# Second-layer attention of a two-layer block: one 32-row strip per head instead of a shared 96-row block

## The chip, the cores and the metric

The kernel runs on one core of a Trainium2 chip. The metric is the time on the device, in microseconds (us), of one execution. Before the change three timed runs gave 1500.37, 1506.84 and 1507.55 us, median 1506.84.

## The reference

The input x has 2048 rows of 128. Four stages follow each other, each added to its input and normalised over the last axis (a layer norm without parameters):

```python
x = LN(x + attn0(x))   # 8 query heads, 2 key groups, causal, latent size 32 per group
x = LN(x + ffn0(x))    # gated FFN, 352 wide, FP4 quantise-dequantise in blocks of 16
x = LN(x + attn1(x))   # below
x = LN(x + ffn1(x))    # 8 experts, weighted by a thresholded softmax
# attn1: H, G, HD = 16, 4, 8
q = (x @ Wq.T + bq).reshape(b, n, G, 4, HD)
k = (x @ Wk.T + bk).reshape(b, n, G, HD)
v = (x @ Wv.T + bv).reshape(b, n, G, HD)
attn = softmax(einsum('bqghd,bkgd->bghqk', q, k) / sqrt(HD))   # not causal
y = einsum('bghqk,bkgd->bqghd', attn, v).reshape(b, n, d) @ Wo.T + bo
```

attn1 has 16 heads of 8 numbers; four heads share the keys of one group. All 2048 queries see all 2048 keys.

## The kernel before

Work goes by chunks of 512 queries (QC) and by key group: a first-layer iteration is (chunk, one of 2 groups), a second-layer iteration (chunk, one of 4 groups), each with four heads. Within an iteration the keys go by tiles of 128. For each tile and head there is a unit: a score matmul (L710) makes scores transposed, 128 keys by 512 queries, in one of three PSUM banks; ScalarE takes the exponential to PR (L903); a product matmul (L728) multiplies by the values, in which a column of ones sums the weights. In the second layer four heads write their products to four strips of 32 rows of one bank, so products come in fours; the trace shows each float32 product as two records. Four units of one key tile with their products are one repeating piece, 16 of them an iteration.

The exponential needs the row maximum. It is found beforehand: for each head, query tile and chunk of keys a matmul (L637, 128 queries by 512 keys) fills one of four side banks, and VectorE reduces it to one column of MP (L1134): 64 such maxima for a second-layer iteration. row_max reduces them further (L1212), a transpose (L642) and a copy bring them to MR, and a DMA (L552) writes them into the last row of the query operand, against which the keys have a row of ones. So the score matmul subtracts the maximum by itself.

For accuracy keys and queries are in two parts, high (rounded to f32r, one pass through TensorE) and low (what is left). The contraction is over high x high, low x high and high x low parts, 3 x 32 rows. In the second layer a group's four heads share the 32 key rows: KO1 holds the 8 key numbers repeated for the four heads, in three parts, 96 rows and the row of ones. A head's own queries are QO rows of its 8 numbers in each part, with the other heads' rows made zero by a mask: q_all (L632) makes all queries of a chunk, ScalarE and VectorE split them to QH and QL (L821, L1123), VectorE copies the group's rows to QB (L1220), and GpSimd multiplies by the head's mask into the query buffer (L968, L971). Queries have four buffers; the fourth lies in KO0, which the second layer no longer needs.

The order of work is written out once as a list of steps (`steps0`, `steps1`, `iteration`, `stream`), and each engine walks the same list in order, with semaphores between them. In an iteration's list each score is followed by the next items beside it: maxima of the coming iteration (it begins a quarter of an iteration after the present one's start and goes on so ahead of its use), and the steps of the FFN or the experts of an earlier chunk. The part list is walked for layer 0, for second-layer chunk 0, in a hardware loop for chunks 1 and 2 (L509), and for chunk 3. The last first-layer iteration and the stretch after it, in which the last chunk's FFN runs, carry the maxima of the first second-layer iterations.

At the start GpSimd fills buffers with constants, among them the rows of ones of KO0 and KO1 (L956, L958), while SyncE issues the loads one by one.

Of the kernel before, what the change touches and what calls it, by code (L numbers as in the profile page):

```python
# [18 lines left out]
P = 128  # L19
T = 2048  # L20
D = 128
NT = T // P
QC = 512
NC = T // QC
QT = QC // P
# [23 lines left out]
CONST_W = 4 * P + 12  # L49


def constants():

    c = np.zeros((P, CONST_W), np.float32)
    i = np.arange(P)
    c[:, 0:P] = np.eye(P)
    c[:, P:2 * P] = np.where(i[:, None] > i[None, :], NEG, 0.0)
    c[:, 2 * P:3 * P] = np.where(i[None, :] > i[:, None], NEG, 0.0)
    for h in range(HG):
        c[:, 3 * P + h] = (i < SHIFT) & ((i % LAT) // HD1 == h)  # L60
    c[:, 3 * P + 4:3 * P + 8] = -0.5
    return c


def build(nc, A):
# [3 lines left out]
    with ctx:  # L69
# [11 lines left out]
        ident, head_mask, minus_half = const[:, 0:P], const[:, 3 * P:3 * P + 4], const[:, 3 * P + 4:3 * P + 8]  # L81
# [6 lines left out]
        KO1 = sb("KO1", [KR, G1, T], f32r)  # L88
        QO = sb("QO", [KR, 3, HG, QC], f32r)

        QBUF = [QO[:, b, :, :] for b in range(3)] + [KO0[:, 0, :].rearrange("p (h q) -> p h q", h=HG)]
        QB = sb("QB", [SHIFT, QC], f32r)
# [46 lines left out]
        WQ1T, WO1T = sb("WQ1T", [P, D]), sb("WO1T", [P, D])  # L139
        QH = sb("QH", [P, QC], f32r)  # L140
        QL = sb("QL", [P, QC], f32r)
        WKV1T = sb("WKV1T", [P, 2 * LAT])
        WK13 = sb("WK13", [P, G1, SHIFT])
        bq = sb("bq", [P, 1])
        bk3 = sb("bk3", [SHIFT, G1])
# [39 lines left out]
        q_base = sem("q_base")  # L185
# [78 lines left out]
        KO = (KO0, KO1)  # L264
# [3 lines left out]
        IN_PARTS = ("q0", "k0", "k1", "q_all")  # L268
        QUANTS = ("quant_x", "quant_h", "quant_w")
        BY_VECTOR = ("norm0", "quant_w", "stats", "final", "q1") + MADE  # L270
# [52 lines left out]
        def stream(part, with_queries=True):  # L323
# [4 lines left out]
            for entry in part:  # L328
# [4 lines left out]
                if with_queries:  # L333
                    asked = (([("q_all", c)] if layer else keys0(c)) if g == 0 else []) + queries(layer, c, g, it)
# [13 lines left out]
        def steps0():  # L348
# [10 lines left out]
            for i, (_, c, g, it) in enumerate(part):  # L359
                beside = between(work, cuts[i], cuts[i + 1]) if i < len(part) - 1 else []  # L360
                if i == len(part) - 1:

                    begun = [step for _, step in behind[1:QUANT_STAGES]]
                    beside = [("q_all", 0)] + begun[:2] + maxima(1, 0, 0, 0, range(NC - 2))
                    begun, behind = begun[2:4] + queries(1, 0, 0, 0) + begun[4:], behind[:1] + behind[QUANT_STAGES:]
# [53 lines left out]
        def name_of(item):  # L419
# [4 lines left out]
            return (kind, item[3]) if kind == "q0" else (kind,)  # L424

        def needs(step):

            kind = step[0]
            if kind == "max":
                _, layer, h, q, kc, c, g, b = step  # L430
                return [("q0", b), ("k0", g)] if layer == 0 else [("k1", g)]
# [5 lines left out]
                    "k1": [("x2T",), ("w1T",)], "v1": [("x2T",)], "q_all": [("x2T",), ("w1T",)],  # L437
# [18 lines left out]
        class Count:  # L456


            def __init__(self, steps):
# [9 lines left out]
                self.groups = kinds.count("q0") + kinds.count("q1")  # L469
                self.bases = kinds.count("q1")  # L470
# [5 lines left out]
            def plus(self, other, times=1):  # L476
# [10 lines left out]
                new.bases = self.bases + other.bases * times  # L487
# [16 lines left out]
        def parts(engine, walk):  # L504
# [4 lines left out]
            with engine.Fori(1, NC - 1) as c:  # L509
# [5 lines left out]
        def _(sp):  # L515
# [15 lines left out]
            sp.dma_start(bq[:, :], A["L1_attn_bq"].rearrange("(r o) -> r o", o=1)).then_inc(ld["attn1"], 16)  # L531
            for r in range(3):
                for j in range(HG):
                    sp.dma_start(bk3[r * LAT + j * HD1:r * LAT + (j + 1) * HD1, :],
                                 A["L1_attn_bk"].rearrange("(g r) -> r g", g=G1), allow_slow_non_contiguous=True).then_inc(ld["attn1"], 16)
# [29 lines left out]
        N_ATTN1 = 16 * (4 + 1 + 3 * HG + 2)  # L565
# [3 lines left out]
        def _(pe):  # L569
            def side_item(item, n, k):  # L570
# [26 lines left out]
                elif kind in ("k0", "k1"):  # L597
                    g, c = item[1:]
                    w = WK3 if kind == "k0" else WK13
                    last = nc.tensor.matmul(bank[0:SHIFT, :], w[:, g, :], XT[:, c * QC:(c + 1) * QC],  # L600
                                            start=True, stop=True)
# [5 lines left out]
                elif kind == "v1":  # L607
                    for j in range(QT):
                        t = item[1] * QT + j
                        last = nc.tensor.matmul(bank[:, j * LAT:(j + 1) * LAT], XT[:, t * P:(t + 1) * P],  # L610
                                                WKV1T[:, LAT:2 * LAT], start=True, stop=True)
# [17 lines left out]
                elif kind == "q_all":  # L629
                    c = item[1]  # L630
                    src = XT[:, c * QC:(c + 1) * QC] if isinstance(c, int) else XT[:, bass.ds(c * QC, QC)]
                    last = nc.tensor.matmul(bank[:, :], WQ1T[:, :], src, start=True, stop=True)  # L632
                elif kind == "max":
                    layer, h, q, kc, c, g, buf = item[1:]
                    n = (q + 1) * P if layer == 0 and kc == c else QC
                    causal = layer == 0 and kc == c
                    last = nc.tensor.matmul(bank[:, 0:n], QBUF[buf][0:SHIFT, h, q * P:(q + 1) * P],  # L637
                                            KO[layer][0:SHIFT, g, kc * QC:kc * QC + n], start=True, stop=not causal)
# [63 lines left out]
            def scores(step, n, u):  # L702
# [7 lines left out]
                m = nc.tensor.matmul(dst[:, q0:QC], KO[layer][:, g, kt * P:(kt + 1) * P], QBUF[buffer_of(layer, it)][:, h, q0:QC],  # L710
# [618 lines left out]
```

## Time and profile before

| | |
|---|---|
| Timed runs | 1500.37, 1506.84, 1507.55 us |
| Span of the profiled execution (no time around it is given) | 1503.6 us |
| Mean granted TensorE clock | 0.937 |
| PE busy (matmul) | 1367.3 us, 91% |
| DVE (VectorE) busy | 1098.1 us, 73% |
| ACT (ScalarE) busy | 827.1 us, 55% |
| POOL (GpSimd) busy | 126.5 us, 8% |

The second layer's attention begins at 634 us of the span and ends at 1463 us; 1415 to 1463 us is its last iteration, where no maxima are left to find. A line of the profile such as L710 is a line of the kernel. PE is the matmul side of TensorE and PEld its weight loads, which overlap. Matmuls are pipelined, so a matmul's duration is longer than the time until the next can begin: the distance between starts tells what one costs. "Idle" before an instruction is the time its engine stood still, and the name behind the arrow is what ended it.

### The profile page before, as it was taken

What the parts mean: (1) busy time and instruction counts of PE and PEld (TensorE: products, weight loads), DVE (VectorE), ACT (ScalarE), POOL (GpSimd) and SP (SyncE); (2) the same over time, 40 slices, a digit from 0 to 9 for tenths busy, and PEclk for the clock granted to TensorE, in tenths of its full rate; (3) what the DMA queues carried; (4) which work ended last, traced back from release to release, by engine and by line L of the source; (5) the groups of instructions that cost most, each with busy time, mean ns of one, the idle gap of its engine ahead of it and who ended that gap; (6) DMA issues with size and microseconds to landing.
All of it is one profiled execution on the core that took longest, in us unless ns stands there. A gap on an engine that the chain in (4) does not pass through costs nothing.

```text
span 1503.6 us, 20967 instructions
## 1 busy us (share of the span) xinstructions
PE 1367.3 (91%) x6537; PEld 697.0 (46%) x6537; DVE 1098.1 (73%) x2178; ACT 827.1 (55%) x1589; POOL 126.5 (8%) x159
## 2 busy tenths in 40 slices
PE   4788899989998965799999999999999999999994
PEld 2444445344433433445555554554554555554432
DVE  4667687678745678778788888887889887887424
ACT  2435534564456511266676666666666666667760
POOL 3000000000000010000000112000121000000033
PEclk9769899899999975799999999999999999999996
DMA  3000000000000000000000000000000000000000
GB/s 101 1 1 1 1 1 2 1 1 1 1 0 1 0 1 0 1 1 1 2 1 1 1 1 9 1 2 3 1 2 8 1 2 2 1 1 1 1 1 14
DMA packets 8785, 6.43 MB, mean 4 GB/s; under 512 B 2072, under 2 KB 7904, under 8 KB 8672
## 3 DMA queue, kind: packets, MB, share of 16 engines
q1 hardware_dynamic: 8672, 5.04, 1.2%
q8 instruction: 57, 0.93, 0.3%
q14 instruction: 56, 0.46, 0.1%
HBM read 3.79 MB, written 1.05 MB: 3 GB/s over the span
## 4 chain that ended last, share of the span: by engine, by line
PE 79%; DVE 13%; ACT 3%; issue 3%; POOL 1%; DMA 0%; DVEq 0%; POOLq 0%; ACTq 0%
PE ps L728 24%; PE ps L710 24%; PE ps L637 19%; DVE MP L1134 6%; PE ps L696 2%; PE ps L600 2%; ACT QO L804 1%; PE ps L663 1%; PE ps L645 1%; PE ps L674 1%; ACT PR L903 1%; PE ps L627 1%; PE ps L648 1%; PE ps L652 1%; PE ps L713 1%
## 5 line engine op out<-in xcount | busy, mean ns | idle before, releaser
L1134 DVE TENSOR_REDUCE MP<-ps 128x1 f32<-128x512 f32 (+2 forms) x1344 | 827.8, 665 | 218.8 <-PE ps L637 185.8
L903 ACT ACTIVATE PR<-ps 128x512 f32<-128x512 f32 (+2 forms) x1344 | 702.0, 584 | 469.8 <-PE ps L710 366.8
L710 PE MATMUL ps<-QO,KO 97*128 97x512 f32 (+3 forms) x1088 | 473.6, 445 | 26.2 <-ACT PR L903 18.3
L637 PE MATMUL ps<-KO,QO 96*128 96x512 f32 (+2 forms) x1088 | 450.1, 437 | 30.8 <-DVE MP L1134 13.1
L728 PE MATMUL ps<-PR,V 128*32 128x512 f32 (+2 forms) x2688 | 432.2, 600 | 0.6 <-ACT OS L804 0.5
L710 PEld LDWEIGHTS ps<-QO,KO 97*128 97x128 f32 x1088 | 208.4, 194 | 339.8 <-ACT PR L903 235.6
L637 PEld LDWEIGHTS ps<-KO,QO 96*128 96x128 f32 x1088 | 219.6, 204 | 91.3 <-DVE MP L1134 39.1
L728 PEld LDWEIGHTS ps<-PR,V 128*32 128x32 f32 (+1 forms) x2688 | 73.7, 115 | 137.5 <-issue 72.0
L710 PE MATMUL ps<-KO 97*128 97x512 f32 x256 | 105.4, 434 | 2.7 <-ACT PR L903 1.5
L637 PE MATMUL ps<-KO 96*128 96x512 f32 x256 | 99.1, 396 | 0.0
L710 PEld LDWEIGHTS ps<-KO 97*128 97x128 f32 x256 | 46.9, 189 | 68.6 <-ACT PR L903 58.1
L963 POOL TENSOR_TENSOR RS<-VE,const 128x4 f32<-128x4 f32 x16 | 16.2, 1013 | 523.1 <-DVE VE L1067 523.1
L968 POOL TENSOR_TENSOR QO<-QB,const 96x512 fp32r<-96x512 f32 x12 | 12.8, 1067 | 530.9 <-DVEq L1223 530.9
L637 PEld LDWEIGHTS ps<-KO 96*128 96x128 f32 x256 | 48.6, 190 | 9.1 <-DVE MP L1134 1.2
L1117 DVE TENSOR_TENSOR QO<-ps,QO 32x512 fp32r<-32x512 f32 x32 | 22.0, 688 | 27.1 <-ACT QO L804 22.8
L980 POOL TENSOR_TENSOR qa<-qa 128x512 f32<-128x512 f32 (+2 forms) x24 | 19.7, 821 | 170.7 <-DVE XQ L1179 166.1
L696 PE MATMUL ps<-ew,XQT 128*128 128x512 f32 x64 | 33.4, 620 | 0.0
L640 PE MATMUL ps<-mask_qk,ident_b 128*128 128x128 bf16 x128 | 33.4, 261 | 0.0
L713 PE MATMUL ps<-mask_kq,ident_b 128*128 128x128 bf16 x128 | 31.8, 248 | 0.0
L804 ACT ACTIVATE HQT<-ps 128x256 f32<-128x256 f32 (+2 forms) x36 | 11.0, 355 | 34.2 <-PE ps L669 31.3
L600 PE MATMUL ps<-XT,WK 128*96 128x512 f32 x48 | 28.7, 700 | 0.0
L669 PE MATMUL ps<-const,H 128*128 128x128 f32 (+1 forms) x48 | 9.8, 319 | 16.2 <-DVEq L1057 15.5
(177 smaller groups left out, 792.0 us busy)
## 6 DMA issues: line engine op xcount, KB each, us to landing
result<-OUT SPq DMA_DIRECT2D x4, 256.0 KB, 2.3
H<-in_L_attn_wq SPq DMA_DIRECT2D x1, 512.0 KB, 6.9
HQT<-in_L_attn_wo SPq DMA_DIRECT2D x1, 512.0 KB, 5.1
ew<-in_L_ffn_expert_w SPq DMA_DIRECT2D x1, 512.0 KB
QO<-MR SPq DMA_DIRECT2D x20, 8.0 KB, 1.8
const<-in_consts SPq DMA_DIRECT2D x1, 262.0 KB, 2.8
bk<-in_L_attn_bk SPq DMA_DIRECT2D x12, 0.1 KB
wd<-in_L_ffn_w_down SPq DMA_DIRECT2D x1, 176.0 KB, 3.6
```

Source lines behind the costliest of these rows:

```text
L600: last = nc.tensor.matmul(bank[0:SHIFT, :], w[:, g, :], XT[:, c * QC:(c + 1) * QC], start=True, stop=True)
L637: last = nc.tensor.matmul(bank[:, 0:n], QBUF[buf][0:SHIFT, h, q * P:(q + 1) * P], KO[layer][0:SHIFT, g, kc * QC:kc * QC + n], start=True, ...
L640: last = nc.tensor.matmul(bank[:, n - P:n], ident_b[:, :], mask_qk[:, :], start=False, stop=True)
L696: last = nc.tensor.matmul(bank[:, :], X2T[:, q * P:(q + 1) * P], ew[:, 4 * e:4 * e + 4, :], start=True, stop=True)
L710: m = nc.tensor.matmul(dst[:, q0:QC], KO[layer][:, g, kt * P:(kt + 1) * P], QBUF[buffer_of(layer, it)][:, h, q0:QC], start=True, stop=not ...
L713: m = nc.tensor.matmul(dst[:, q0:q0 + P], ident_b[:, :], mask_kq[:, :], start=False, stop=True)
L728: nc.tensor.matmul(dst, VO[layer][:, kt, g, :], PR[:, u % NP_RING, q0:QC], start=kt == 0, stop=kt == key_tiles(layer, c) - 1).then_inc(pv_ ...
L804: return nc.scalar.activation(out, in_, ACT.Copy)
L903: nc.scalar.activation(PR[:, u % NP_RING, q0:QC], ps[:, 8 - nb + u % nb, q0:QC], ACT.Exp, scale=SCALE[layer]).then_inc(exp_done, 1)
L980: nc.gpsimd.tensor_tensor(t[:, 0:w, :], t[:, 0:w, :], t[:, w:2 * w, :], ALU.add).then_inc(pool_chain, 1)
L1117: i = v.tensor_tensor(q[2 * LAT:SHIFT, :], bank[h * LAT:(h + 1) * LAT, :], q[0:LAT, :].bitcast(f32), ALU.subtract)
L1134: v.tensor_reduce(MP[:, buf, h, q, kc:kc + 1], bank[:, 0:w], AX, ALU.max).then_inc(free, 1)
```

## The change

Each second-layer head gets a strip of 32 partitions of its own, in keys (KO1, now 128 rows) and in queries (Q1, 128 rows by 4 groups): 8 numbers in three parts, 24 rows, and a 25th row for the ones (keys) and the shift (queries). The weights WK13 and WQ13 are laid out so that one matmul per group makes all four strips; ScalarE writes the high parts and zeros (a per-partition scale of 0 or 1), VectorE the tails. A maximum contracts 24 rows of its strip, a score 25. The maxima of the second layer are emitted with the head innermost. The masked queries, QB, QH, QL and q_all go; q1 becomes a step of its own per group, with a bank. The shift goes by four DMAs, one a strip. The bias comes by 24 small DMAs. The hardware loop over chunks 1 and 2 is written out.

```diff
-CONST_W = 4 * P + 12
+PARTS1 = 3 * HD1
+ROWS1 = PARTS1 + 1
+CONST_W = 3 * P + 10
...
+    c[:, 3 * P + 4] = (i % LAT) // HD1 == 1
+    c[:, 3 * P + 5] = (i % LAT) // HD1 == 2
+    c[:, 3 * P + 6:3 * P + 10] = (i % LAT == PARTS1)[:, None]
...
-        KO1 = sb("KO1", [KR, G1, T], f32r)
+        KO1 = sb("KO1", [P, G1, T], f32r)
+        Q1 = sb("Q1", [P, G1, QC], f32r)
...
-            return [("max", layer, h, q, kc, c, g, buffer_of(layer, it)) for h in range(HG) for q in range(QT)
-                    for kc in chunks or range(top)]
+            if layer == 1:
+                return [("max", 1, h, q, kc, c, g, it) for q in range(QT) for kc in chunks or range(NC) for h in range(HG)]
...
-            with engine.Fori(1, NC - 1) as c:
+            for c in range(1, NC - 1):
...
-                        dst = QBUF[step[3]][SHIFT:KR, :, :].rearrange("o h (q p) -> o (h q) p", p=P)
-                        sp.dma_start(dst.bitcast(f32), MR[:, :].bitcast(f32)).then_inc(shifted, 16)
+                            for h in range(HG):
+                                row = h * LAT + PARTS1
+                                dst = Q1[row:row + 1, step[3], :].rearrange("o (q p) -> o q p", p=P)
+                                sp.dma_start(dst.bitcast(f32), MR[h * QT:(h + 1) * QT, :].bitcast(f32)).then_inc(shifted, 16)
...
+                elif kind == "q1":
+                    g, c, _ = item[1:]
+                    last = nc.tensor.matmul(bank[:, :], WQ13[:, g, :, :], XT[:, c * QC:(c + 1) * QC], start=True, stop=True)
+                elif kind == "max" and item[1] == 1:
+                    _, h, q, kc, c, g, buf = item[1:]
+                    rows = slice(h * LAT, h * LAT + PARTS1)
+                    last = nc.tensor.matmul(bank[:, :], Q1[rows, buf, q * P:(q + 1) * P], KO1[rows, g, kc * QC:(kc + 1) * QC],
+                                            start=True, stop=True)
...
-                m = nc.tensor.matmul(dst[:, q0:QC], KO[layer][:, g, kt * P:(kt + 1) * P], QBUF[buffer_of(layer, it)][:, h, q0:QC],
-                                     start=True, stop=not causal)
+                    rows = slice(h * LAT, h * LAT + ROWS1)
+                    m = nc.tensor.matmul(dst[:, :], KO1[rows, g, kt * P:(kt + 1) * P], Q1[rows, it, :], start=True, stop=True)
...
+                        i = nc.scalar.activation(Q1[:, item[3], :], bank, ACT.Identity, bias=bq_low[:, g:g + 1], scale=low_q)
...
+                        i = nc.scalar.activation(KO1[:, item[1], item[2] * QC:(item[2] + 1) * QC], bank, ACT.Identity,
+                                                 bias=bk_low[:, item[1]:item[1] + 1], scale=low_k)
...
+            nc.gpsimd.memset(WQ13[:, :, :, :], 0.0)
+            nc.gpsimd.memset(WK13[:, :, :, :], 0.0)
...
-            nc.gpsimd.memset(KO1[SHIFT:KR, :, :].bitcast(f32), 1.0).then_inc(ones_set, 1)
+            nc.gpsimd.memset(UNUSED[:, :], 0.0).then_inc(ones_set, 1)
...
-            def masked(n, buf):
-
-                pool.wait_ge(q_base, n)
-                nc.gpsimd.tensor_tensor(QBUF[buf][0:SHIFT, 0, :], QB[:, :].bitcast(f32),
-                                        head_mask[0:SHIFT, 0:1].broadcast_to([SHIFT, QC]), ALU.mult)
...
+                    tails(KO1[:, item[1], item[2] * QC:(item[2] + 1) * QC], bank, bk13[:, item[1]:item[1] + 1]).then_inc(free, 1)
+                elif kind == "q1":
+                    tails(Q1[:, item[3], :], bank, bq13[:, item[1]:item[1] + 1]).then_inc(free, 1)
...
-                    for part, src in enumerate((QH, QH, QL)):
-                        i = v.tensor_scalar(QB[part * LAT:(part + 1) * LAT, :], src[g * LAT:(g + 1) * LAT, :].bitcast(f32),
-                                            1.0, None, ALU.mult)
```

## Rows read from the trace of the kernel before

**Rows 1.** The page, busy us (share of the span) and count by engine.
```profile
PE 1367.3 (91%) x6537; PEld 697.0 (46%) x6537; DVE 1098.1 (73%) x2178; ACT 827.1 (55%) x1589; POOL 126.5 (8%) x159
```
**Rows 2.** Stretches: length, busy PE, PEld, DVE, ACT, POOL, clock, DMA share, GB/s.
```profile
650.00:1415.00 765.00, 753.84 (x3930) 388.57 (x3925) 628.32 (x1107) 508.05 (x982) 68.04 (x89) 1.00 0.01 2
...
534.00:640.00 106.00, 68.44 (x203) 40.09 (x202) 81.92 (x188) 17.82 (x32) 5.07 (x6) 0.67 0.00 0
```
**Rows 3.** The chain of waits, 650 to 1463 us, shares by line.
```profile
by line: PE ps L710 32.9%; PE ps L728 29.2%; PE ps L637 24.8%; DVE MP L1134 3.1%; PE ps L696 2.5%; issue 1.8%; PE ps L645 0.7%; ACT PR L903 0.5%; DVE QB L1220 0.5%; PE ps L692 0.4%; PE ps L656 0.3%; DVE ST L1062 0.3%; PE ps L632 0.3%; PE ps
```
**Rows 4.** By shape, 650 to 1415 us: count | busy us, mean ns | idle.
```profile
L1134 DVE TENSOR_REDUCE MP<-ps 128x1 f32<-128x512 f32 x909 | 566.6, 684 | 112.0 <-PE ps L637 108.2
L903 ACT ACTIVATE PR<-ps 128x512 f32<-128x512 f32 x941 | 494.9, 600 | 247.5 <-PE ps L710 243.9
```
**Rows 5.** Timeline (start us, length us) of a piece with four maxima.
```profile
1244.15 1.06 PE L728 MATMUL ps<-PR,V 128*32 128x512 f32 x8
...
1245.15 0.50 PE L710 MATMUL ps<-KO 97*128 97x512 f32 x1
...
1245.49 0.40 PE L637 MATMUL ps<-KO,QO 96*128 96x512 f32 x1
...
1245.92 1.89 DVE L1134 TENSOR_REDUCE MP<-ps 128x1 f32<-128x512 f32 x3 [0.21 <-PE ps L637]
...
1246.89 0.39 PE L637 MATMUL ps<-KO,QO 96*128 96x512 f32 x1
...
1247.21 0.64 PE L728 MATMUL ps<-PR,V 128*32 128x512 f32 x4
```
**Rows 6.** Timeline of a piece without maxima.
```profile
1459.78 1.07 PE L728 MATMUL ps<-PR,V 128*32 128x512 f32 x8
...
1460.78 0.98 PE L710 MATMUL ps<-KO 97*128 97x512 f32 x3
...
1461.97 0.50 PE L710 MATMUL ps<-KO 97*128 97x512 f32 x1 [0.21 <-ACT PR L903]
...
1462.40 1.06 PE L728 MATMUL ps<-PR,V 128*32 128x512 f32 x8
```
**Rows 7.** DVE, 650 to 1463 us: stretch of L1220 alone, then L1123.
```profile
650.00:1463.00 813.00, 16.31 (x39) 1.00 0.01 2
...
L1123 DVE SCALAR_TENSOR_TENSOR QL<-ps,bq,QH 128x512 fp32r<-128x512 f32 x3 | 2.3, 751 | 3.0 <-ACT QH L821 3.0
```
**Rows 8.** By shape, whole span; then L632's matmuls, min/median/max ns.
```profile
L1081 DVE SCALAR_TENSOR_TENSOR KO<-ps,bk,KO 32x512 fp32r<-32x512 f32 x16 | 11.9, 743 | 10.8 <-ACT KO L828 9.2 <-PE ps L600 1.2
...
L632 PE MATMUL ps<-XT,WQ1T x6: 590/592/595, 730.4 to 1168.5; 128*128 x4, 128*128 128x512 f32 x2
```
**Rows 9.** What DVE waited for, 650 to 1415 us: total, times, longest.
```profile
DVE MP L1134 <- PE ps L637: 108.2, 187, 3.2
```
**Rows 10.** Timeline of the start.
```profile
8.52 6.96 POOL L958 MEMSET KO<- 1x8192 f32 x1
...
11.70 4.96 DVE L1305 COPY WK<-wkd 128x32 f32<-128x32 f32 x6
...
16.98 1.94 PE L584 MATMUL ps<-const,H 128*128 128x128 f32 x8 [7.60 <-DVEq L1306]
```
**Rows 11.** Timeline at the loop's edge and at the last shift.
```profile
1048.83 0.49 PE L710 MATMUL ps<-QO,KO 97*128 97x512 f32 x1 [2.68 <-issue]
...
1413.49 0.50 SPq L552 DMA_DIRECT2D KO<-MR  x1
1415.30 0.53 PEld L710 LDWEIGHTS ps<-KO 97*128 97x128 f32 x3 [2.05 <-DMA KO<-MR]
```
**Rows 12.** Timeline of PE from 634 us.
```profile
634.28 0.76 PE L710 MATMUL ps<-QO,KO 97*128 97x512 f32 x1 [1.37 <-DVE UNUSED L1142]
634.85 0.63 PE L637 MATMUL ps<-KO,QO 96*128 96x512 f32 x1
635.27 0.63 PE L710 MATMUL ps<-QO,KO 97*128 97x512 f32 x1
```

More of the change, by code:

```diff
@@ L333, in stream @@
                 if with_queries:
-                    asked = (([("q_all", c)] if layer else keys0(c)) if g == 0 else []) + queries(layer, c, g, it)
+                    asked = (keys0(c) if layer == 0 and g == 0 else []) + queries(layer, c, g, it)
                 lead = before * QUERY_LEAD
@@ L363, in steps0 @@
                     begun = [step for _, step in behind[1:QUANT_STAGES]]
-                    beside = [("q_all", 0)] + begun[:2] + maxima(1, 0, 0, 0, range(NC - 2))
-                    begun, behind = begun[2:4] + queries(1, 0, 0, 0) + begun[4:], behind[:1] + behind[QUANT_STAGES:]
+                    beside = queries(1, 0, 0, 0) + begun[:2] + maxima(1, 0, 0, 0, range(NC - 2))
+                    begun, behind = begun[2:], behind[:1] + behind[QUANT_STAGES:]
                 yield from iteration(0, c, g, beside, behind, outs, carry, it, begun)
@@ L430, in needs @@
                 _, layer, h, q, kc, c, g, b = step
[L431 removed]
+                return [("q0", b), ("k0", g)] if layer == 0 else [("q1", b), ("k1", g)]
             return {"fold_q": [("wqT", 0), ("wqT", 1), ("wupT",)], "fold_o": [("wupT",)],
@@ L468, in __init__ @@
                 self.outs = kinds.count("out_copy")
-                self.groups = kinds.count("q0") + kinds.count("q1")
-                self.bases = kinds.count("q1")
+                self.groups = kinds.count("q0")
                 self.shifts = kinds.count("shift")
@@ L530, in _ @@
             sp.dma_start(Wkv1[LAT:2 * LAT, :], A["L1_attn_Wv"]).then_inc(ld["attn1"], 16)
[L531 to L535, printed above, removed]
+            sp.wait_ge(consts_set, 1)
+            for h in range(HG):
+                for r in range(3):
+                    rows = slice(h * LAT + r * HD1, h * LAT + (r + 1) * HD1)
+                    sp.dma_start(bq13[rows, :], A["L1_attn_bq"].rearrange("(g h d) -> h d g", g=G1, h=HG)[h],
+                                 allow_slow_non_contiguous=True).then_inc(ld["attn1"], 16)
+                    sp.dma_start(bk13[rows, :], A["L1_attn_bk"].rearrange("(g d) -> d g", g=G1),
+                                 allow_slow_non_contiguous=True).then_inc(ld["attn1"], 16)
             for dst, name, n in ((bv_b, "L1_attn_bv", LAT), (bo_b, "L1_attn_bo", D)):
@@ L628, in side_item @@
                                             start=True, stop=True)
[L629 to L632, printed above, removed]
+                elif kind == "q1":
[5 more added lines that the diff above has]
+                    last = nc.tensor.matmul(bank[:, :], Q1[rows, buf, q * P:(q + 1) * P], KO1[rows, g, kc * QC:(kc + 1) * QC],
+                                            start=True, stop=True)
                 elif kind == "max":
                     layer, h, q, kc, c, g, buf = item[1:]
[L635 to L638, printed above, removed]
+                    n = (q + 1) * P if kc == c else QC
+                    causal = kc == c
+                    last = nc.tensor.matmul(bank[:, 0:n], QO[0:SHIFT, buf, h, q * P:(q + 1) * P],
+                                            KO0[0:SHIFT, g, kc * QC:kc * QC + n], start=True, stop=not causal)
                     if causal:
@@ L709, in scores @@
                 dst = ps[:, 8 - nb + u % nb, :]
-                m = nc.tensor.matmul(dst[:, q0:QC], KO[layer][:, g, kt * P:(kt + 1) * P], QBUF[buffer_of(layer, it)][:, h, q0:QC],
-                                     start=True, stop=not causal)
+                if layer == 0:
+                    m = nc.tensor.matmul(dst[:, q0:QC], KO0[:, g, kt * P:(kt + 1) * P], QO[:, buffer_of(0, it), h, q0:QC],
+                                         start=True, stop=not causal)
+                else:
+                    rows = slice(h * LAT, h * LAT + ROWS1)
+                    m = nc.tensor.matmul(dst[:, :], KO1[rows, g, kt * P:(kt + 1) * P], Q1[rows, it, :], start=True, stop=True)
                 if causal:
@@ L768, in walk @@
                             its += 1
-                            pe.wait_ge(shifted, 16 * (n.iterations + its + 1))
+                            pe.wait_ge(shifted, 64 * (n.iterations + its + 1))
                         scores(step, n, u)
@@ L777, in walk @@
                         pe.wait_ge(out_free, n.outs + outs)
-                    if kind == "max" and step[7] in q_at:
+                    if kind == "max" and step[1] == 0 and step[7] in q_at:
                         pe.wait_ge(q_ready, q_at.pop(step[7]))
@@ L991, in walk @@
                         rstd(n.rstd + rs)
-                    if kind == "q1":
-                        bases += 1
-                        masked(n.bases + bases, step[3])
                     if kind in ("expert", "ebias"):
@@ L1074, in normalise, with tails @@
                 return i
-            def tails(dst, tail, bank, bias=None):
-                lo = slice(tail * LAT, (tail + 1) * LAT)
-                if bias is None:
-                    return v.tensor_tensor(dst[lo, :], bank[lo, :], dst[lo, :].bitcast(f32), ALU.subtract)
-                return v.scalar_tensor_tensor(dst[lo, :], bank[lo, :], bias[lo, :], dst[lo, :].bitcast(f32), ALU.add,
-                                              ALU.subtract)
+            def tails(dst, bank, bias):
+                return v.scalar_tensor_tensor(dst, bank, bias, dst.bitcast(f32), ALU.add, ALU.subtract)
             def chunk_of(c):
```

119 lines of the change are left out of this document (54 added, 65 removed).

## Prediction

> **What bounds the kernel now.** I read the page first, then the second layer alone, then one repeating piece of it instruction by instruction. The page has TensorE (PE) at 91% and VectorE (DVE) at 73% [rows 1]. The change touches the second-layer attention, so the stretches come next [rows 2]: from 650 to 1415 us, where the maxima of coming queries run beside the scores, PE is busy 753.8 of 765 us at full clock, DVE 628.3, ScalarE (ACT) 508.1. The chain of waits over 650 to 1463 us is PE almost alone: scores (L710) 32.9%, products (L728) 29.2%, maxima (L637) 24.8%; the DVE reduction has 3.1% [rows 3]. So PE bounds this layer, and DVE is next, 137 us behind.
>
> The stretch has 941 exponentials, one per score unit, hence 235 pieces of four units ("quads": four scores, some maxima, four products), 765/235 = 3.26 us each; its 909 reductions make 3.9 a quad [rows 4]. One quad with four maxima [rows 5]: products start at 1244.15, the first score at 1245.15 (1.00 us later), its neighbour 0.34 later, then a score or maximum each 0.233 us (1245.49 to 1246.89 are six such steps), and products again at 1247.21, 0.32 after the last maximum: 3.06 us, and nothing in it waits. The reader is to see that eight score and maximum matmuls cost PE about 1.9 us, although each contracts 96 or 97 rows of which a head's own are 24.
>
> **The change, part by part.**
>
> *Strips.* After it, a score or maximum uses the 32 rows of its head's strip, and the emission order of the maxima puts the four heads next to each other. Does PE run strips side by side? The trace has no matmul that contracts a strip. It has the other direction: products write 32 output rows each, and four records take 0.64 us, eight 1.06 [rows 5], so four run together. Bounds for one S or M matmul in a strip: 0.233 us as now (no overlap; gain nothing), down to a quarter of it, 0.06. Scores walk heads 0 to 3, maxima too but at a shifted phase, so in the worst case a maximum sits behind a score of its own strip and pairs with the next score: five steps of 0.233 for eight matmuls, 1.17 us. I take overlap, anywhere from pairs to fours; PE then needs at most 1.00 + 0.34 + 3 x 0.233 + 0.32 = 2.4 us a quad, and it stops being the bound.
> The Trainium skill (TensorE: Matmul & The Clock Gate, Part 3: Packing small matmuls) says that matmuls in different 32-row strips run concurrently, four of them 3.07 times as fast; by it the eight would cost 8 x 0.233/3.07 = 0.6 us, an estimate from that page. No row here shows it; it speaks against the second rival below.
>
> *What is late next.* Two things. First the loop between PE and ACT: a score needs one of three banks. The quad without maxima shows it bare [rows 6]: products at 1459.78, three scores from 1460.78, the fourth at 1461.97 after 0.21 us of idle on the first exponential, products at 1462.40: 2.62 us. Row strips don't shorten this, so 2.62 is the floor of every quad. Second DVE: three reductions in 1.89 us with 0.68 for the last, so one each 0.60 us [rows 5]; four are 2.4 us, five 3.0.
> DVE's own work changes too. The three copies per group to QB (L1220: 16.3 us in this layer) and the QL tails (3 x 0.75 = 2.3) go [rows 7]; one tail per group comes, 13 x 0.74 at the price of the key tail L1081 [rows 8] = 9.7. So 628.3 - 16.3 - 2.3 + 9.7 = 619.4 us, 2.64 a quad: the two limits are equal on average, and the time lies above both because maxima come unevenly. DVE idles 137 us now, 108.2 of it waiting for a maximum [rows 9]. The other 28.5 (side chains through PE, ACT, GpSimd) stay. The uneven part I estimate: at 3.9 on average with threes, fours and fives, about a quarter of the quads (60) carry three maxima or fewer; DVE then idles 2.62 - 3 x 0.60 - 0.2 (side work) = 0.6 us, 60 x 0.6 = 36, and 4 us for quads whose other side matmuls hold PE. Sum 619.4 + 28.5 + 40 = 688, against 765: **-77 us**. Ends: 0 (no overlap), and -146 (DVE never idle).
>
> *1415 to 1463 us*, no maxima, 16 quads at 3.0 us: they are at the floor or hold expert matmuls with all 128 rows. -2 (0 to -6).
>
> *Query production.* GpSimd's four masking operations per group go; GpSimd is busy 68 of 765 us [rows 2], so that is worth nothing. The masked queries' wait goes; what is next is the DVE tail, a quad early at least. PE does 16 query matmuls instead of 4, each two records of 0.59 us [rows 8], begun 0.43 apart as such two-pass records are (the products' second four end 0.42 after the first) [rows 5]: +12 x 0.86 = 10 us of PE; ACT +12 at the length of an exponential, 0.60 [rows 4], is 7. Both now have slack under DVE; each can hold up a quad a little. +2 (0 to +10).
>
> *Switching between array shapes.* Layer 1's maxima are also issued in the last first-layer iteration and from 534 to 640 us, between matmuls that use 128 rows. The one shape change that the trace shows costs 0.32 - 0.233 = 0.09 us on entry to the products [rows 5]. Some 110 maxima, two changes each, 20 us of PE at most; from 534 to 640 PE is busy 68 of 106 us and DVE 82 [rows 2], which hides nearly all. +2 (0 to +20).
> The Trainium skill (TensorEngine Tiling (Array Packing), Key Properties) has the rule against this change: changing the tiling mode drains TensorE. The trace agrees as far as the 0.09 us goes. The products already differ in shape from the scores, so inside the layer the number of changes a quad stays two; by the rule the extra ones are those just priced.
>
> *Start.* The memset of 8192 ones on GpSimd (6.96 us) goes, two of 512 columns come, by the same price 6.96/16 = 0.44 each, and two tiny ones, 1 us. While it runs, six small copies of DVE take 4.96 us; PE waits 7.60 us for the last of them [rows 10]. The copies begin at 11.70; without the memset beside them I take 0.2 us each, an estimate, so they end near 13 instead of 16.7: -4 (0 to -5). The additional bias DMAs (24 for 13) are waited for only after this.
>
> *Loop unrolled.* At 1048.83 PE had stood 2.68 us with nothing to wait for [rows 11], once; -2 (0 to -3).
>
> *Four shift DMAs for one.* SyncE issues each in 0.50 us; exposed only where the last group's shift is late (issued 1413.49, score 1415.30) [rows 11]: 3 x 0.5 = +1.5. Elsewhere a shift has a quarter of an iteration ahead of its use.
>
> Sum: -77 - 2 + 2 + 2 - 4 - 2 + 1.5 = -79.5, on a span of 1503.6 us: 1424. The page gives no time around the span; the median of the timed runs, 1506.84, is 3.2 above it. Predicted 1427 us.
>
> **The rivals.**
> 1. *DVE becomes the bound, as above*: 1427, own range 1385 to 1465. For it: DVE is the only engine close behind. Chance 72%.
> 2. *The change doesn't do what it says*: strips are computed one after another. Then every S and M still costs 0.233, PE stays the bound, only the start, loop, added query matmuls and switches count: -4 - 2 + 10 + 2 + 1.5 = +7, with DVE's relief worth nothing: 1514, or 1504 if the added matmuls hide. For it: no row shows strips overlapping. Against: products overlap by columns. 10%.
> 3. *Partial gain through one queue*: PE issues in order, so a maximum waiting for DVE holds the next score back, and that score's exponential comes late. Both loops then add up in part, and a quad costs some 3.1 us instead of 2.93: 235 x 0.15 = 35 gained, 1469 with the small terms, up to 1490. For it: score and maximum alternate in the queue. Against: four side banks cover 4 x 0.60 = 2.4 us, more than the 1.3 us of products. 9%.
> 4. *Slower: the clock falls.* Throughout 650 to 1463 us PE is busy and the granted clock is 1.00 (2.4 GHz); from 534 to 640, where PE idles a third of the time, it is 0.67 on average [rows 2]. After the change PE would work perhaps 1.9 of 2.9 us. At 1.2 GHz a step is 0.42 us (634.85 to 635.27) and the first after a pause 0.57 (634.28 to 634.85) [rows 12]; the products' 1.00 would be 1.9, twice its 0.85 of streaming, and the 0.32 after the last maximum 0.5, both estimates. A quad in pairs: 1.9 + 0.57 + 3 x 0.42 + 0.5 = 4.2 us, against 2.93. It decides from (3.26 - 2.93)/(4.2 - 2.93) = a quarter of the quads on; at half of them, 235 x (0.5 x 1.27 - 0.33) = +72, some 1576 with the small terms. Against: a slow PE is a fully busy one, and from 650 us on the clock is full though the stretch ahead was not [rows 2]. 9%.
>
> **How the numbers follow.** Faster by over 0.5% (about what a measurement of this kernel can tell from no change): case 1, case 3 and a third of case 2, 84%. Within 0.5%: most of the rest of case 2, 6%. Slower: case 4 and a little of case 2, 10%. The range for 8 in 10 runs from 1385 (more than half of the way to DVE never idle) to 1490, which takes in case 3.
>
> **What would show it.** Maxima and scores starting a few ns apart in groups, at durations near 0.4 us; DVE near 90% busy where it was 82%, its waits for maxima from 108 to some 40 us; L637 and L710 gone from the head of the chain in favour of the reduction; quads without maxima still at 2.62 us; PE clock 1.00; PE's start on the weights near 13 us. The forecast is wrong if scores and maxima keep a pitch of 0.23 us, if the clock line shows halves after 650 us, or if DVE still waits over 80 us for maxima with PE idle.

## The result: 15.8% slower, at a lower TensorE clock

The changed kernel takes 1759.84 us (median of four runs: 1742.04, 1744.34, 1775.35, 1780.00) where the one before has 1505.49 (four runs). The ratio is 1.158, 95% interval 1.154 to 1.161; ratios here leave out runs well above the fastest of the same kernel, which are the two longer ones here (granted clock 0.68 where the others have 0.71), 1525.95 and 1530.01 us in e7 below, and 3654.64 us in e8. The forecast was 1427 us. What happened is rival 4, the falling clock, to which I gave 9%.

The page of the changed kernel, busy times by engine, its slices (tenths, 40 of them over the span) and the chain by line:

```profile
PE 1549.5 (89%) x6565; PEld 578.7 (33%) x6565; DVE 1081.3 (62%) x2149; ACT 840.0 (48%) x1602; POOL 71.6 (4%) x99
...
PE   4889899999997679999889999999999999998895
...
PEclk8688898999998566555775655655565565578586
...
PE ps L747 30%; PE ps L730 19%; ACT PR L921 7%; PE ps L726 5%; DVE MP L1138 4%; PE ps L652 4%; PE ps L646 3%; PE ps L711 3%; PE ps L642 2%; PE ps L660 1%; ACT QO L823 1%; PE ps L678 1%; PE ps L611 1%; PE ps L689 1%; POOL qc L990 1%
```

Against [rows 1], PE is busy 182 us longer with the same number of matmuls, give or take 28. Read alone, that says that PE is slower. The PEclk line says where. A slice is 43.5 us. In the first 13 slices, up to 566 us, it is 8 or 9 but for one 6; from there on it is 5 to 7 but for two slices of 8 near the end. The second layer begins at some 640 us; the stretch just ahead of it is at a low clock in both kernels (0.67 before, 0.65 after). (Products are now L747, scores of the second layer L730, its maxima L646, the reduction L1138.)

The stretches answer to [rows 2]: length, busy PE, PEld, DVE, ACT, POOL, granted clock, DMA share, GB/s.

```profile
650.00:1415.00 765.00, 717.29 (x3052) 214.96 (x3050) 482.92 (x845) 398.27 (x763) 27.43 (x36) 0.60 0.01 2
...
534.00:640.00 106.00, 69.89 (x208) 36.36 (x206) 80.61 (x183) 17.15 (x31) 2.01 (x2) 0.65 0.00 1
...
855.00:880.00 25.00, 20.79 (x153) 6.22 (x149) 22.71 (x38) 19.49 (x39) 0.00 (x0) 1.00 0.01 1
680.00:850.00 170.00, 161.74 (x642) 44.55 (x640) 94.33 (x156) 85.90 (x166) 0.00 (x0) 0.52 0.00 1
...
1541.00:1599.00 58.00, 49.52 (x346) 16.60 (x346) 50.96 (x86) 44.95 (x88) 0.00 (x0) 1.00 0.01 1
```

The same 765 us hold 763 ScalarE instructions where they held 982 [rows 2]. The clock is 0.60 where it was 1.00. The last three rows are the key: in the 25 us from 855, at full clock, DVE is busy 91%, as forecast (near 90%); in the 170 us from 680, at 0.52, it is 55%. The longest stretch at full clock, 58 us from 1541, has DVE at 88%; PE is busy only 85% of it, and the clock stays full.

A quad at full clock and one at half, from the timeline (start us, length us). First full:

```profile
1588.79 1.06 PE L747 MATMUL ps<-PR,V 128*32 128x512 f32 x8
1589.79 0.49 PE L730 MATMUL ps<-Q,KO 25*128 25x512 f32 x1
1589.79 0.50 PE L646 MATMUL ps<-KO,Q 24*128 24x512 f32 x1
1589.79 0.53 PE L730 MATMUL ps<-Q,KO 25*128 25x512 f32 x2
1590.12 0.40 PE L646 MATMUL ps<-KO,Q 24*128 24x512 f32 x2
1590.97 0.49 PE L730 MATMUL ps<-Q,KO 25*128 25x512 f32 x1 [0.44 <-ACT PR L921]
1591.38 1.07 PE L747 MATMUL ps<-PR,V 128*32 128x512 f32 x8
```

Then half:

```profile
1103.03 1.94 PE L747 MATMUL ps<-PR,V 128*32 128x512 f32 x8
1104.90 0.80 PE L730 MATMUL ps<-Q,KO 25*128 25x512 f32 x3
1105.49 0.64 PE L646 MATMUL ps<-KO,Q 24*128 24x512 f32 x3
1106.38 0.79 PE L730 MATMUL ps<-Q,KO 25*128 25x512 f32 x1 [0.25 <-ACT PR L921]
1107.10 1.08 PE L747 MATMUL ps<-PR,V 128*32 128x512 f32 x4
```

In the first, three scores and a maximum begin in one moment (1589.79) and last 0.5 us: strips do run side by side. The quad, with three maxima, is 2.59 us long, and PE stands still 0.44 us on ACT. In the second, three scores last 0.80 us together and three maxima 0.64, PE stands still 0.25 us on ACT, and products begin at 1103.03 and again at 1107.10, 4.07 us apart. Counted on the timeline over the whole second layer, from one set of products to the next: 67 quads at full clock with a mean of 2.87 us, 160 at half with 4.69, 27 with a change inside. Counted in the same way, the kernel before has 253 of 254 at full clock, with a mean of 3.24 us.

### The profile page after: what moved, and what is told of

It reads as the page before. It is cut to its first block, busy times and chain, and to the rows that moved or that the text cites. A ratio compares the mean times of both kernels' runs of the same rounds, so it can differ in the third digit from the quotient of the medians.

```text
span 1740.3 us, 19160 instructions
## 1 busy us (share of the span) xinstructions
PE 1549.5 (89%) x6565; PEld 578.7 (33%) x6565; DVE 1081.3 (62%) x2149; ACT 840.0 (48%) x1602; POOL 71.6 (4%) x99
## 4 chain that ended last, share of the span: by engine, by line
PE 76%; DVE 10%; ACT 9%; issue 3%; POOL 1%; DMA 1%; SPq 1%; DVEq 0%; POOLq 0%; ACTq 0%
PE ps L747 30%; PE ps L730 19%; ACT PR L921 7%; PE ps L726 5%; DVE MP L1138 4%; PE ps L652 4%; PE ps L646 3%; PE ps L711 3%; PE ps L642 2%; PE ps L660 1%; ACT QO L823 1%; PE ps L678 1%; PE ps L611 1%; PE ps L689 1%; POOL qc L990 1%
## 5 line engine op out<-in xcount | busy, mean ns | idle before, releaser
L1138 DVE TENSOR_REDUCE MP<-ps 128x1 f32<-128x512 f32 (+2 forms) x1344 | 827.6, 664 | 389.7 <-PE ps L646 306.8
L747 PE MATMUL ps<-PR,V 128*32 128x512 f32 (+2 forms) x2688 | 585.4, 839 | 0.6 <-ACT OS L823 0.6
L730 PE MATMUL ps<-Q,KO 25*128 25x512 f32 x1024 | 412.6, 668 | 68.6 <-ACT PR L921 60.8
L646 PE MATMUL ps<-KO,Q 24*128 24x512 f32 x1024 | 411.8, 635 | 16.6 <-DVE MP L1138 12.7
L730 PEld LDWEIGHTS ps<-Q,KO 25*128 25x128 f32 x1024 | 157.9, 253 | 578.6 <-issue 297.6
L646 PEld LDWEIGHTS ps<-KO,Q 24*128 24x128 f32 x1024 | 170.9, 262 | 55.2 <-DVE MP L1138 36.6
L726 PE MATMUL ps<-QO,KO 97*128 97x512 f32 (+3 forms) x320 | 148.8, 475 | 20.5 <-ACT PR L921 18.4
L652 PE MATMUL ps<-KO,QO 96*128 96x512 f32 (+2 forms) x320 | 137.1, 465 | 16.4 <-DVE QO L1120 13.0
L747 PEld LDWEIGHTS ps<-PR,V 128*32 128x32 f32 (+1 forms) x2688 | 81.5, 133 | 161.8 <-ACT PR L921 104.9
L726 PEld LDWEIGHTS ps<-QO,KO 97*128 97x128 f32 x320 | 63.9, 203 | 148.7 <-ACT PR L921 91.2
L652 PEld LDWEIGHTS ps<-KO,QO 96*128 96x128 f32 x320 | 69.0, 221 | 29.7 <-DVE QO L1120 14.1
L642 PE MATMUL ps<-XT,WQ 128*128 128x512 f32 x32 | 30.6, 1056 | 0.0
```

The lines of the kernel that those rows point to most:

```text
L642: last = nc.tensor.matmul(bank[:, :], WQ13[:, g, :, :], XT[:, c * QC:(c + 1) * QC], start=True, stop=True)
L646: last = nc.tensor.matmul(bank[:, :], Q1[rows, buf, q * P:(q + 1) * P], KO1[rows, g, kc * QC:(kc + 1) * QC], start=True, stop=True)
L652: last = nc.tensor.matmul(bank[:, 0:n], QO[0:SHIFT, buf, h, q * P:(q + 1) * P], KO0[0:SHIFT, g, kc * QC:kc * QC + n], start=True, stop=not ...
L726: m = nc.tensor.matmul(dst[:, q0:QC], KO0[:, g, kt * P:(kt + 1) * P], QO[:, buffer_of(0, it), h, q0:QC], start=True, stop=not causal)
L730: m = nc.tensor.matmul(dst[:, :], KO1[rows, g, kt * P:(kt + 1) * P], Q1[rows, it, :], start=True, stop=True)
L747: nc.tensor.matmul(dst, VO[layer][:, kt, g, :], PR[:, u % NP_RING, q0:QC], start=kt == 0, stop=kt == key_tiles(layer, c) - 1).then_inc(pv_ ...
```

## The experiments

Each is the changed kernel with one edit unless it says otherwise. The table gathers what they say of the clock. "Stretch" is 650 to 1415 us; "PE busy" is out of its 765 us.

| run | second-layer matmuls | span us | PE busy | clock in the stretch |
|---|---|---|---|---|
| before | 96 and 97 rows, one after another | 1503.6 | 753.8 | 1.00 |
| e5 | before, 64 rows | 1828.3 | 760.1 | 0.62 |
| e3 | before, 32 rows | 2006.5 | 761.7 | 0.57 |
| after | strips of 24 and 25 rows | 1740.3 | 717.3 | 0.60 |
| e4 | strips, maxima in the old order | 1839.8 | 755.8 | 0.56 |
| e9 | strips, 2 zero matmuls of 32 rows a quad | 1545.1 | 741.7 | 0.82 |
| e11 | same, 128 rows, 32 output rows | 1514.0 | 745.5 | 0.95 |
| e6 | same, 1 over the whole array | 1566.5 | 715.8 | 0.85 |
| e1 | same, 2 over the whole array | 1502.5 | 733.6 | 0.98 |
| e2 | same, 4 over the whole array | 1582.1 | 741.5 | 1.00 |

**e1_fill2, e2_fill4, e6_fill1: work for the whole array.**

```diff
+        FILL = sb("FILL", [P, P + QC], bf16)          # weights 0.0, moving data 1.0
...
+                if layer == 1 and h == 3 and kt != 1 and (c, g, kt) != (0, 0, 0):
+                    for _ in range(2):                # e6: 1, e2: 4
+                        nc.tensor.matmul(ps[:, OUT_BANKS[0], :], FILL[:, 0:P], FILL[:, P:P + QC], start=False, stop=False)
```

> The changed kernel with two matmuls of zero weights over all 128 rows (128x128 by 128x512, bfloat16) added before every fourth score of the second layer; they add zero to the output bank. Theory A (the second layer is slow because TensorE is granted 1.2 GHz while its matmuls use one strip each, and for nothing else): the clock returns to near 1.00 from 650 us on, a quad takes 2.8 to 3.0 us, span 1430 to 1490 us. Theory B (the clock falls because TensorE stands still between its matmuls, waiting for ScalarE and VectorE, whatever rows it uses): the same, since the idle time is filled; told from A by the rows run below. Theory C (strips and changes of array shape cost time by themselves, the clock is a side effect): 240 x 2 x 0.43 us more than the changed kernel, about 1900 us.

> As before, with four such matmuls before every fourth score. Theories A and B: clock 1.00, but four cost 0.9 us where some 0.45 us of slack stands before the fourth score, so a quad is about 3.2 us and the span 1500 to 1540 us, slower than with two if two suffice. Theory C: above 2000 us.

> The changed kernel with one zero matmul over all rows before every fourth score instead of two. If the work of the rows sets the grant, one is between none (0.57) and two (0.98): clock 0.75 to 0.95 in 650 to 1415 us, span 1520 to 1620 us. If one is enough, a quad is as long as with two or 0.1 us shorter, span 1480 us.

Measured, one run each: 1504.3, 1583.9 and 1568.3 us, beside 1508.4 us (one run, for the first two) and 1507.0 us (median of 15, for the third) for the kernel before. Adding about 480 matmuls that compute nothing takes 238 us off the span. This is the experiment that settles what slowed the change: the clock goes from 0.60 to 0.98 and the time with it. The stretch in e1:

```profile
650.00:1415.00 765.00, 733.63 (x4436) 239.74 (x4509) 626.39 (x1100) 533.06 (x1023) 28.48 (x37) 0.98 0.01 2
```

A quad with two of them, at full clock:

```profile
1227.20 1.06 PE L751 MATMUL ps<-PR,V 128*32 128x512 f32 x8
1228.20 0.49 PE L734 MATMUL ps<-Q,KO 25*128 25x512 f32 x1
...
1228.87 0.61 PE L725 MATMUL ps<-FILL 128*128 128x512 bf16 x2
1229.40 0.49 PE L734 MATMUL ps<-Q,KO 25*128 25x512 f32 x1
...
1230.07 1.06 PE L751 MATMUL ps<-PR,V 128*32 128x512 f32 x8
```

They stand where PE waited for ACT: the fourth score begins 1.20 us after the first, and did so after 1.18 in the full-clock quad without them. This quad, with two of its five maxima beside the fourth score, is 2.87 us. With four the clock is full, but its 247 full-clock quads have a mean of 3.45 us against the 3.24 of the kernel before, so e2 is 75 us slower than that one, and my 1500 to 1540 us was missed. With one, the clock is 0.85, within the 0.75 to 0.95 expected: full-clock quads have a mean of 2.95 us (193 of 254), and 45 at half clock with 5.15 lose it. Theory C, that shapes or strips are slow by themselves, falls. My figure for e1, 1430 to 1490, was missed: quads that carry experts, transposes or a query projection already fill PE, and there the zero matmuls only add. Counted on e1's timeline, its 242 full-clock quads have a mean of 3.08 us, where the kernel before has 3.24; of the other 12, six at half clock have a mean of 6.3 us and six with a change inside 5.0.

**e3_rows32 and e5_rows64: the old kernel with fewer rows.**

```diff
-                    last = nc.tensor.matmul(bank[:, 0:n], QBUF[buf][0:SHIFT, h, q * P:(q + 1) * P],
-                                            KO[layer][0:SHIFT, g, kc * QC:kc * QC + n], start=True, stop=not causal)
+                    kr = 32 if layer == 1 else SHIFT      # e5: 64; scores alike
+                    last = nc.tensor.matmul(bank[:, 0:n], QBUF[buf][0:kr, h, q * P:(q + 1) * P],
+                                            KO[layer][0:kr, g, kc * QC:kc * QC + n], start=True, stop=not causal)
```

> The kernel before, with the second layer's maxima and scores contracting only rows 0 to 31 (the low parts and the shift are left out). All lie in the same strip, so nothing overlaps and TensorE is as busy in time as before, 0.233 us a matmul. Theory A (the grant goes by how many rows of the array work): the clock falls from 1.00 to about 0.5 to 0.7 after 650 us, span 1700 us or more, even above the changed kernel, since nothing overlaps: 8 x 0.43 + 1.9 = 5.3 us a quad if always at 1.2 GHz. Theory B (it goes by the time in which TensorE stands still): TensorE never waits, the clock stays 1.00, span 1500 us.

> The kernel before, with the second layer's maxima and scores contracting rows 0 to 63 (the second low part and the shift are left out). Time per matmul is as before, 0.233 us at full clock, nothing overlaps. If the grant goes by how many rows of the array work, 64 lie between 96 (clock 1.00) and 32 (0.57 in 650 to 1415 us): I expect 0.8 to 1.0 there, span 1500 to 1700 us. If only matmuls confined to one 32-row strip count less, it is 1.00 and 1500 us.

Measured, one run each, 2008.3 and 1830.2 us, beside 1508.4 and 1507.0. The number, order and columns of the matmuls are those of the kernel before. What is contracted differs in content too: the low parts (in e5 one of them) and the row of the shift are left out. Zeros in the array don't lower the clock, as e1 with its zero weights shows, so I take the number of rows as the cause. Where the clock is full, a step costs what it did (e3, timeline):

```profile
1245.03 0.39 PE L638 MATMUL ps<-KO 32*128 32x512 f32 x1
1245.26 0.38 PE L712 MATMUL ps<-QO,KO 32*128 32x512 f32 x1
```

and yet over the stretch (e3):

```profile
650.00:1415.00 765.00, 761.73 (x2399) 357.92 (x2398) 409.64 (x685) 341.11 (x600) 44.83 (x59) 0.57 0.00 1
```

PE is busy 761.7 of 765 us, and is granted 1.2 GHz for most of it. So a fully occupied instruction stream doesn't hold the clock; how many rows its matmuls use counts. Weight loads don't explain it either: PEld is busy 357.9 us in e3, at a clock of 0.57, and 239.7 us in e1, at 0.98. The Trainium skill (TensorE: Matmul & The Clock Gate, section What's actually happening) says that the clock gate is set by how busy the PE has been; here the measurement decides that busy by the trace's rows is not the quantity. For e5 I had written 0.8 to 1.0 or, by the other reading, 1.00; both are missed, 64 rows gave 0.62, so it isn't proportional to rows.

**e9_fill2_strip and e11_fill2_cols: which part of the array.** The zero matmuls of e1 on FILL[0:LAT] only, and on all rows with 32 output rows (shortened).

```diff
-  nc.tensor.matmul(ps[:, OUT_BANKS[0], :], FILL[:, 0:P], FILL[:, P:P + QC], ...)
+  nc.tensor.matmul(ps[:, OUT_BANKS[0], :], FILL[0:LAT, 0:P], FILL[0:LAT, P:P + QC], ...)      # e9
+  nc.tensor.matmul(ps[0:LAT, OUT_BANKS[0], :], FILL[:, 0:LAT], FILL[:, P:P + QC], ...)        # e11
```

> The changed kernel with two zero matmuls before every fourth score as in the run with two over all rows, same columns and same place, but contracting only 32 rows (the first strip). They fill TensorE's time in the same way. If the grant goes by how many rows work, the clock stays where the changed kernel has it (0.5 to 0.65 in 650 to 1415 us) and the time is that of the changed kernel plus 240 x 2 x 0.3 to 0.43 us: 1850 to 1950 us. If it goes by TensorE's idle time, the clock comes back to near 1.00 as with all rows, 1500 us.

> The changed kernel with two zero matmuls before every fourth score that contract all 128 rows but make only 32 output rows (a quarter of the array's columns, as the products do). With all rows and columns two gave a clock of 0.98 in 650 to 1415 us, with 32 rows and all columns 0.82, with none 0.60. If a matmul counts by the part of the array it fills, rows times columns, this gives 0.82 as the 32-row ones do, span 1540 us. If only the rows count, 0.98 and 1500 us. If it is the time filled that counts, all three should have been alike, which they are not.

Measured, one run each, 1546.9 and 1515.8 us, beside 1508.4 and 1506.0. The stretch in e9:

```profile
650.00:1415.00 765.00, 741.68 (x4191) 243.92 (x4187) 595.37 (x1045) 488.39 (x943) 28.43 (x37) 0.82 0.01 2
```

and in e11:

```profile
650.00:1415.00 765.00, 745.50 (x4449) 235.46 (x4441) 622.25 (x1087) 524.71 (x1007) 28.47 (x37) 0.95 0.01 2
```

e9 is against my theory: two matmuls in one strip, a quarter of the array, put where PE stood still, brought 0.60 to 0.82, when I expected 0.5 to 0.65 (and near 1.00 if idle time were the cause). So filled time counts too, beside rows. e11, at 0.95, lies between e9 and e1, where I had expected 0.82 or 0.98: 128 rows by 32 columns did more than 32 rows by 128, though both are a quarter of the array, so by these two runs "rows times columns" falls as well. No rule of mine fits all of the table: e3 has the least idle time and the lowest clock but one, e9 has less full-array work than e6 and nearly its clock. These are single runs, and the grant varies from run to run (0.68 to 0.71 over the whole span in the changed kernel, 0.892 to 0.914 in e10 below). What exactly is counted stays open, and with it how much of the changed kernel's low clock comes from its few rows and how much from its idle time.

**e4_old_order: strips with the old order of maxima.**

```diff
-  ... for q in range(QT) for kc in chunks or range(NC) for h in range(HG)]
+  ... for h in range(HG) for q in range(QT) for kc in chunks or range(NC)]
```

> The changed kernel with the maxima in the order of before (head outermost), so that sixteen maxima in a row lie in one strip and overlap with scores only. Theory A: the clock stays low, little changes in the grant; overlap is less, so a quad costs more, span 1750 to 1900 us. Theory B: TensorE has less idle time, so the clock is higher than in the changed kernel, span under 1700 us.

Measured, one run, 1841.6 us beside 1508.4, within the 1750 to 1900 expected; clock 0.56, PE busy 755.8 of 765 instead of 717.3: less idle time, and no higher clock. The head-inner order, by which more matmuls overlap, is worth 60 to 100 us at the low clock (the changed kernel's runs are 1742 to 1780). That goes with e3, and against idle time as the whole cause, by which I had expected a higher clock and under 1700 us.

**e8_small_parts: the kernel before with two side effects of the change alone.**

```diff
-            with engine.Fori(1, NC - 1) as c:
+            for c in range(1, NC - 1):
...
+            pool.wait_ge(weights_ready, 1)
             nc.gpsimd.memset(KO1[SHIFT:KR, :, :].bitcast(f32), 1.0).then_inc(ones_set, 1)
```

> The kernel before with only two side effects of the change: the hardware loop written out, and the memset of 8192 ones issued once the first weight copies are done, so that it no longer runs beside them. Expected -4.0 us at the start (TensorE's wait for the copies ends at 12.9 instead of 17.0 us) and -2 us at the loop's edge: 1498 to 1502 us, ratio 0.996. If the start's gain is lost later in the first layer, ratio 0.999.

Measured 1497.12 us (median of six), ratio 0.994 (0.992 to 0.997). The start in e8, timeline:

```profile
12.45 1.26 DVE L1306 COPY WK<-wkd 128x32 f32<-128x32 f32 x6 [3.73 <-DMA HQT<-in_L_attn_wo]
13.88 6.92 POOL L959 MEMSET KO<- 1x8192 f32 x1 [5.44 <-DVEq L1307]
```

Six small copies take 1.26 us instead of the 4.96 of [rows 10] once GpSimd isn't at its memset beside them. Set beside the trace of before, e8's product matmuls begin 4.5 us earlier at 160 us, 6.1 earlier at the start of the second layer and 6.7 just ahead of the chunk's edge at 1048 us, 8.8 behind it. The start and the loop's edge are thus each seen in the trace, at 4.5 and 2.1 us; the 1.5 us at 640 us are not explained.

**e7, e10, e12: can the strips be kept and the clock with them?** e7 is e1 with four zero matmuls in the last iteration. e10 leaves them out where PE had other full-row work:

```diff
+                    n_fill = 0 if aside[0] else 3 if (c, g) == (NC - 1, G1 - 1) else 2
+                    aside[0] = 0
...
+                    aside[0] += kind not in ("max", "shift", "pad")
```

and e12 keeps them in the first four key tiles of each chunk nevertheless (`if aside[0] and (g or kt > 3)`).

> With two zero matmuls a quad the clock still fell in the last iteration, where no maxima are left (half clock for 37 of its 74 us). Four there, two elsewhere: if the clock is the cause of that iteration's length, it takes 50 to 60 us instead of 74 and the span is 1480 to 1492 us; if the four matmuls cost as much as the clock gives back, 1500 us as with two.

> The changed kernel with two zero matmuls over all rows before every fourth score, but none where another matmul over all rows (transpose, projection, expert) was issued since the last such place; three in the last iteration. If those other matmuls keep the clock up by themselves, some 50 quads get 0.4 us shorter and the clock stays near 0.98: 1475 to 1485 us, ratio 0.98. If they do not, the clock falls in the expert stretches and the time is 1500 to 1540 us.

> The adaptive version (zero matmuls left out where another matmul over all rows was issued), but with the two zero matmuls kept also in the first four key tiles of each chunk's first iteration, where the clock fell in the adaptive run (at 838, 1046 and 1254 us, 51 us at half clock in all). If these falls are due to the zero matmuls left out there, the clock is 0.98 to 1.00 in 650 to 1415 us, 1470 to 1485 us, ratio 0.98, and the spread of the runs (1484 to 1506) shrinks. If the falls come from TensorE standing still at the chunk's edge, nothing changes: ratio 0.992.

Measured, medians of ten runs each: e7 1502.45 us, ratio 0.996 (0.994 to 0.998); e10 1497.68, ratio 0.992 (0.989 to 0.996); e12 1508.1, ratio 0.9995 (0.997 to 1.002). All three miss what was expected (1480 to 1492 us of span for e7, where the profiled run has 1496.5; 1475 to 1485 for e10; 1470 to 1485 for e12). In e7 the last 16 quads' products begin within 55.2 us where e1 has 61.7 and the kernel before 44.2, so more filling gave back over a third of that iteration's loss. e10 is faster than both kernels, with the lowest single time, 1483.94, but is scattered up to 1505.83, and over its runs time goes with the clock: 1483.94 at 0.912, 1505.83 at 0.894. Its stretch:

```profile
650.00:1415.00 765.00, 742.86 (x4498) 241.31 (x4495) 627.61 (x1106) 537.51 (x1036) 28.45 (x37) 0.97 0.01 2
```

e12 has more of the zero matmuls than e10 and a lower clock (0.94 in its stretch), against what I expected of them. It ran on another chip than e10; whether the chip or the edit made the difference wasn't separated. As a gain, e10 isn't told from e8 (0.994), which has none of the strips.

## Why the prediction was wrong, step by step

- **The failed step is the clock, which the sum holds at 1.00 in every quad, on rival 4's "Against" and its 9%.** Measured, it is 0.60 from 650 to 1415 us, and 160 of 254 quads ran at half clock, at 4.69 us where the sum has 2.93. I wrote that a slow PE is a fully busy one and that from 650 us on the clock is full though the stretch ahead was not. Both read PE's busy time as what earns the clock. In every row of before busy time and full rows went together (96 and 97 rows, products over 128), so the trace couldn't tell them apart, and I took the one that let the change win. e3 shows that busy time alone doesn't earn it (761.7 of 765 us busy, clock 0.57), and e1 that giving the array work brings the time back. Rival 4 named only idle time as the cause. The number of rows, which e3 and e5 show to matter, stood nowhere in the prediction, and for 58 us the clock stayed full with PE busy 85%. So rival 4 was right that the clock could fall, and only in part right about why.
- **Its price came out right, in part by luck.** Rival 4 said 4.2 us for a quad in pairs at 1.2 GHz; 68 quads at half clock with four maxima and no matmul over all 128 rows and columns have a mean of 4.20. But its terms are not those of the trace: the strips overlap by more than pairs, and the quad shown is 1.87 us of products, 1.48 until the fourth score, which waits for ACT, and 0.72 until the next products. It said that half of the quads at 1.2 GHz would give 1576; nearly two thirds were, and those with query or expert matmuls take 5 to 6 us, which I had left out.
- **Strips overlap.** Right, by fours even (1589.79). The Trainium skill (TensorE: Matmul & The Clock Gate, Part 3: Packing small matmuls) says that matmuls in different 32-row strips run concurrently. The trace agrees: at 1104.90 three scores in three strips take 0.80 us together, where one takes 0.79.
- **The two limits at full clock.** Right in the short stretches that had it: DVE 22.71 of 25.00 us busy (forecast: near 90%), and the floor between PE and ACT is 2.59 to 2.61 us (forecast 2.62). The mean quad at full clock is 2.87 us, against the 2.93 of the sum. No run shows this over the whole layer: in e1, at 0.98, DVE is busy 626.4 of 765 us, as before the change, and PE still heads the chain. A sum with the mean can be made: the 254 quads hold 1048 us; at 2.87 they would be 729, 319 less, and the span 1421 against the 1424 forecast. This is worked out, not run, and it is kind: the full-clock quads of this run had fewer other matmuls among them.
- **Start.** Right: PE begins at 12.94 us instead of 16.98, -4.0.

PE's start on the weights, changed kernel:

```profile
11.36 1.27 DVE L1302 COPY WK<-wkd 128x32 f32<-128x32 f32 x6 [1.64 <-DMA HQT<-in_L_attn_wo]
...
12.94 1.94 PE L592 MATMUL ps<-const,H 128*128 128x128 f32 x8 [3.80 <-DVEq L1303]
```

- **The other small terms** (switching shapes, query matmuls, shift DMAs) are below what the clock did, and weren't tried one by one; e8 gives -8.6 us for start and loop edge together, forecast -6, which lies within its interval.
- **DVE's wait** for maxima (L1138 on L646) is 210.9 us in the stretch against the 108.2 of [rows 9], the sign named for a wrong forecast, as the halves in the clock line are. In e1 (L1144 on L647), with the clock back, it is 71.0, where the forecast was some 40.

The waits, total, times and longest, first of the changed kernel and then of e1:

```profile
DVE MP L1138 <- PE ps L646: 210.9, 152, 2.9
...
DVE MP L1144 <- PE ps L647: 71.0, 125, 2.5
```

## What to carry to other kernels

A change that makes matmuls smaller or lets them overlap must be priced at both clocks, and the chance of the low one can't be read from how busy TensorE looks: ask which rows of the array would still be at work. Before trusting the gain, run the old kernel with fewer rows; it costs one line in the maxima and one in the scores, and e3 and e5 would have shown the low clock before the change was written. When TensorE is already near its neighbours' pace, the largest gain that it can give is small beside what half the clock takes, and filling with empty work gives most of the loss back but little of the gain.

## What the runs showed of the hardware that I had not expected

- Contracting 32 rows instead of 96 and 97, at the same columns, order and number of matmuls, lowered the granted clock from 1.00 to 0.57 of 2.4 GHz (650 to 1415 us) and made the kernel 500 us longer; 64 rows gave 0.62. In the kernel before, the full clock was held although the mask makes 72 of a head's 96 query rows zero, where e4, with the same 24 rows a head that aren't zero and PE as busy, had 0.56. So rows of zeros count as well, as the zero weights of e1 do.
- Some 480 zero-weight matmuls of bfloat16, two a quad, brought the clock from 0.60 to 0.98 when they used the whole array, to 0.95 with 128 rows and 32 columns, and to 0.82 in one strip.
- A GpSimd memset of one partition by 8192 slowed small VectorE copies beside it from 0.21 to 0.83 us each, and a 128x128 cast from 0.21 us (changed kernel, without the memset beside it) to 7.03 (the trace of before).
